# Layer-0 attention of a two-layer transformer: each head pair's projection and norm bound, and the ternary quantisation of the FFN weights, moved into the attention loops

## The reference

```
x = x + attn0(layernorm(x))   # qkv = x @ Wqkv.T + bqkv; 16 heads of 64; softmax(q k^T / 8) v; @ Wo.T + bo
x = x + ffn0(layernorm(x))    # gelu(x @ T(W1).T + b1) @ T(W2).T + b2
x = x + attn1(layernorm(x))   # Taylor feature map, causal
x = x + ffn1(layernorm(x))    # silu gate, int weights

def _ternary(w):              # T above; W1 is (4096, 1024), W2 is (1024, 4096)
    scale = jnp.maximum(jnp.mean(jnp.abs(w)), 1e-08)
    w_t = jnp.clip(jnp.round(w / scale), -1.0, 1.0)
```

## Time and profile before

| | us |
|---|---|
| median of 2 runs | 4363.91 (4304.0 to 4423.83) |
| the profiled execution, its own time | 4297.45 |
| its span on the slowest core (core 1) | 4295.9 |
| spans of the 8 cores | 4277.5 to 4295.9 |
| TensorE busy | 2523.8 (59%) |
| VectorE busy | 1594.5 (37%) |
| ScalarE busy | 1177.2 (27%) |

### The profile page before, as it was taken

One profiled execution on the slowest core, in us unless ns is written; L12 is line 12 of the kernel. 1 busy time (PEld: TensorE's weight loads), 2 busy tenths in 40 slices (PEclk: granted clock), 3 DMA queues, 4 the chain that ended last, 5 costly groups with the idle time before them and its releaser, 6 DMA issues. The chain is left out here.

```text
span 4295.9 us, 38629 instructions; the slowest of 8 cores (4277.5 to 4295.9 us)
## 1 busy us (share of the span) xinstructions
PE 2523.8 (59%) x12136; PEld 1064.5 (25%) x12136; DVE 1594.5 (37%) x3449; ACT 1177.2 (27%) x1691; POOL 110.4 (3%) x162
## 2 busy tenths in 40 slices
PE   1466565655656465000179996585555572779777
PEld 0112121121221112000034442243333340234333
DVE  2423324243232424645410003247777754231231
ACT  1162442615335162000231222213333332111110
POOL 0000000000000000111000000000000000001000
PEclk8687787867777687555589997785555576999999
DMA  4000000000000001756133321110000000636226
GB/s 113 8 1 8 0 8 8 0 8 1 8 0 1 0 1 69 262 193 201 57 88 74 74 59 20 30 20 1 1 1 1 1 1 7 87 59 75 45 39 123
DMA packets 178929, 188.11 MB, mean 44 GB/s; under 512 B 118432, under 2 KB 159408, under 8 KB 175024
## 3 DMA queue, kind: packets, MB, share of 16 engines
q0 software_dynamic: 90400, 126.92, 14.1%
q1 hardware_dynamic: 88336, 58.72, 4.9%
HBM read 211.85 MB, written 25.17 MB: 55 GB/s over the span
## 5 line engine op out<-in xcount | busy, mean ns | idle before, releaser
L52 ACT ACTIVATE SCR<-S,NEGC 128x1024 bf16<-128x1024 f32 x512 | 548.4, 1112 | 151.4 <-PE S L52 147.6
L52 PE MATMUL PO<-SCR,VP 128*65 128x512 bf16 x1024 | 346.5, 423 | 168.4 <-ACT SCR L52 92.8
L52 DVE CAST Y<-PO 64x512 bf16<-64x512 f32 x64 | 43.7, 683 | 630.1 <-PE PO L52 629.7
L52 DVE TENSOR_TENSOR X<-X,TF 128x512 f32<-128x512 f32 x64 | 44.3, 693 | 583.4 <-ACT TF L52 583.4
L52 PE MATMUL lnA<-lnXB,ONES_B 128*1 128x512 bf16 x128 | 56.8, 623 | 342.6 <-ACT lnXB L52 342.6
L52 PE MATMUL PGU<-XLN,WGS 128*128 128x512 bf16 x768 | 182.8, 381 | 119.0 <-DVE HH L52 93.7
L52 PE MATMUL PH<-XLN,W1S 128*128 128x512 bf16 x1024 | 223.0, 381 | 16.8 <-DMA W1S<-w1b 15.7
L52 PE MATMUL PH<-HSB,W2S 128*128 128x512 bf16 x1024 | 221.3, 379 | 1.9 <-ACT HSB L52 1.9
L52 PE MATMUL S<-QP,KP 64*128 64x512 bf16 x1024 | 216.4, 430 | 5.1 <-DVE NEGC L52 5.1
L50 DVE RECIPROCAL DROW<-DROW 1x512 bf16<-1x512 bf16 x64 | 206.6, 3292 | 0.8
L52 PE MATMUL PAUX<-DROW,ONES_B 1*64 1x512 bf16 x64 | 38.4, 599 | 284.7 <-DVE DROW L50 232.4
(11 more groups left out here) (157 smaller groups left out, 3787.5 us busy)
## 6 DMA issues: line engine op xcount, KB each, us to landing
WSL<-w POOLq DMA_DIRECT2D x16, 2048.0 KB, 11.6
WSL<-w POOLq DMA_DIRECT2D x64, 512.0 KB, 4.2
W1S<-w1b SPq DMA_DIRECT2D x16, 1024.0 KB, 5.3
W2S<-w2b SPq DMA_DIRECT2D x16, 1024.0 KB, 6.8
WGS<-wg POOLq DMA_DIRECT2D x12, 1024.0 KB, 8.9
WUS<-wu POOLq DMA_DIRECT2D x12, 1024.0 KB, 13.2
WDS<-wd POOLq DMA_DIRECT2D x16, 768.0 KB, 8.3
w1b<-WTB SPq DMA_DIRECT2D x8, 1024.0 KB, 4.5
```

What stands on the lines that cost most here:

```text
L52: ins = getattr(e, meth)(*a, **kw)
```

## The change

1. The steps ahead of the attention of a pair (projections, squares, norm matmuls, NEGC) become a generator `prep_chunks(pr)`, cut into 20 chunks: 8 for Q/K (one group each), 4 for V (four tiles each), 1 for the squares, 4 for the norms (four matmuls each), 3 for the chain to NEGC.
2. The ternary work becomes a generator `ternary_chunks()`: for each weight 8 chunks of four slabs of absolute sums, 3 for the threshold, 16 of two slabs of compare and write, 54 in all and a last empty one. W1 too is now cut into 32 slabs of 128x1024. Stage `p2a` is gone.
3. `pump()` appends one chunk to the engines' lists: of the next pair's preparation as long as there is any, else of the ternary work. It is called after each of the 17 steps of each `qc` block and after each of the 8 rounds of the tail, so 76 times a pair. Pair 0's own preparation is appended whole, ahead of the loop.
4. Everything that the chunks put into PSUM goes to the one bank PAUX; each use waits for VectorE's copy of the one before (`paux_free_vs`). The copies of Q and K move from ScalarE to VectorE. The squares get their own place in SCR, NEGC two buffers. The tail's broadcast matmuls use PO instead of PAUX.
5. The first block loads only pair 0's weights; pair pr + 1's are issued when the preparation of pair pr starts. WO0 is loaded inside `p2`, whose matmuls wait for it.

```diff
-    WO0 = sbuf("WO0", [128, 8 * 1024], BF16, es0a)
-    for i in range(2):
-        p.dma("gpsimd", WQP[i][:, :], dram["wq0"][i], dc)
...
+    p.dma("gpsimd", WQP[0][:, :], dram["wq0"][0], dc)
...
-    p.dma("gpsimd", WO0[:, :], dram["wo0"], dc)
...
+            def prep_chunks(pr):
                 pb = pr % 2
+                if pr + 1 < 8:
+                    p.wait("gpsimd", ts, trk["wread_ts"][1 - pb])
+                    p.dma("gpsimd", WQP[1 - pb][:, :], dram["wq0"][pr + 1], dwp[1 - pb])
...
+                for which in range(2):
+                    WB = WQP[pb] if which == 0 else WKP[pb]
...
                     for tc in range(NT):
+                        p.wait("tensor", vs, trk["paux_free_vs"])
                         for c in range(NFC):
+                            p.op("tensor", "matmul", PAUX[:, :], WB[:, c * 128:(c + 1) * 128],
                                  XLN[:, c * T + tc * 512: c * T + tc * 512 + 512],
...
+                        p.wait("vector", ts)
                         if which == 0:
+                            p.op("vector", "tensor_scalar", DSTT[:, tc * 512:(tc + 1) * 512],
+                                 PAUX[:, :], 0.125, BQ8[:, pr:pr + 1], AL.mult, AL.add,
+                                 inc=vs)
...
+                        trk["paux_free_vs"] = vs.n
+                        yield pr
                 for tt in range(NTT):
+                    p.wait("tensor", vs, trk["paux_free_vs"])
+                    p.op("tensor", "matmul", PAUX[:, 0:128], ONES_B[0:1, 0:128],
...
+                    trk["paux_free_vs"] = vs.n
+                    if tt % 4 == 3:
+                        yield pr
...
+                            p.wait("tensor", vs, trk["paux_free_vs"])
+                            p.op("tensor", "matmul", PAUX[0:1, 0:512], NRM2[:, aa:aa + 1],
...
+            def ternary_chunks():
+                w1q = dram["w1"].rearrange("c p (q f) -> c q p f", f=1024)
...
+                    nslab = 32
+                    p.wait("gpsimd", vs)
+                    p.dma("gpsimd", WSL[0][:, :], wdram(0), dsl[0])
+                    p.dma("gpsimd", WSL[1][:, :], wdram(1), dsl[1])
+                    for s_ in range(nslab):
+                        p.wait("vector", dsl[s_ % 2])
+                        p.op("vector", "reduce_sum", RACC[:, s_:s_ + 1], WSL[s_ % 2][:, :],
+                             axis=AX.X, apply_absolute_value=True, inc=vs)
+                        if s_ + 2 < nslab:
+                            p.wait("gpsimd", vs)
+                            p.dma("gpsimd", WSL[s_ % 2][:, :], wdram(s_ + 2), dsl[s_ % 2])
+                        if s_ % 4 == 3:
+                            yield 99
...
+                    for s_ in range(nslab):
+                        p.wait("vector", dsl[s_ % 2])
...
+                        if s_ % 2 == 1:
+                            yield 99
...
+            def pump(n=1):
+                for _ in range(n):
+                    if cur_prep[0] is not None:
+                        try:
+                            next(cur_prep[0])
+                            continue
+                        except StopIteration:
+                            cur_prep[0] = None
+                    if not tern_done[0]:
+                        try:
+                            next(tern)
+                        except StopIteration:
+                            tern_done[0] = True
+
+            for _ in prep_chunks(0):
+                pass
+
+            for pr in range(8):
+                pb = pr % 2
+                cur_prep[0] = prep_chunks(pr + 1) if pr + 1 < 8 else None
...
+                            exp_ss[(kt)] = ss.n
+                        pump()
+                    trk["last_exp_ss"] = exp_ss[NKT - 1]
...
+                        p.op("tensor", "matmul", PO[0:64, 0:512], ONES_B[64:65, 0:64],
                              DROW[64:65, g * 512:(g + 1) * 512], start=True, stop=True,
...
+                        p.op("vector", "tensor_mul", yslc, yslc, PO[0:64, 0:512], inc=vs)
+                        trk["zmul_vs"] = vs.n
+                        pump()
...
+            p.dma("gpsimd", WO0[:, :], dram["wo0"], dc)
+            p.wait("tensor", dc)
...
-    if act("p2a"):
```

More of the change, by code:

```diff
@@ L465, in build_program @@
                 sq_vs = vs.n
-                aux_v = vs.n
+                yield pr
                 p.wait("tensor", vs, sq_vs)
-                p.wait("tensor", vs, zmul_vs)
                 for which, SRC in enumerate([QS, KS]):
-                    for a in range(2):
+                    for aa in range(2):
                         for tc in range(NT):
[L472 to L476, removed]
+                            g = (which * 2 + aa) * NT + tc
+                            p.wait("tensor", vs, trk["paux_free_vs"])
+                            p.op("tensor", "matmul", PAUX[0:1, 0:512], NRM2[:, aa:aa + 1],
+                                 SRC[:, tc * 512:(tc + 1) * 512], start=True, stop=True,
+                                 inc=ts)
                             p.wait("vector", ts)
@@ L530, in build_program @@
                             if pk == 0:
[L531 to L535, removed]
+                                p.wait("tensor", vs, trk["o_evac_vs"])
+                                p.wait("tensor", vs, trk["zmul_vs"])
+                            for aa in range(2):
+                                p.op("tensor", "matmul", PO[:, aa * 512:(aa + 1) * 512],
+                                     VP[pb][:, pk * 130 + aa * 65: pk * 130 + aa * 65 + 65],
+                                     PSB[pk % 2][:, aa * 512:(aa + 1) * 512],
                                      start=(pk == 0), stop=(pk == NKT - 1),
-                                     inc=(ts if a == 1 else None))
+                                     skip_group_check=True,
+                                     inc=(ts if aa == 1 else None))
                             pv_ts[pk] = ts.n
@@ L564, in build_program @@
                 for qc in range(NT):
[L565 to L566 removed]
+                    for aa in range(2):
+                        g = qc * 2 + aa
                         p.wait("tensor", vs, zr_vs)
[L568 to L569 removed]
+                        p.wait("tensor", vs, trk["zmul_vs"])
+                        p.op("tensor", "matmul", PO[0:64, 0:512], ONES_B[64:65, 0:64],
                              DROW[64:65, g * 512:(g + 1) * 512], start=True, stop=True,
[L571 removed]
+                             skip_group_check=True, inc=ts)
                         zb_t = ts.n
                         p.wait("vector", ts, zb_t)
[L574 to L582 removed]
+                        yslc = Y[64 * aa:64 * aa + 64, pr * T + qc * 512: pr * T + qc * 512 + 512]
+                        p.op("vector", "tensor_mul", yslc, yslc, PO[0:64, 0:512], inc=vs)
+                        trk["zmul_vs"] = vs.n
+                        pump()
+                while cur_prep[0] is not None:
+                    pump()
+            while cur_prep[0] is not None or not tern_done[0]:
+                pump()
             p.emit(nc)
```

260 lines of the change are left out of this document (117 added, 143 removed).

## The result

| | before | after |
|---|---|---|
| median of all executions (10 and 11) | 4358.78 | 4492.34 |
| lowest | 4299.40 | 4357.28 |
| ratio, with its 95% interval | | 1.0135 (1.0117 to 1.0153) |
| the profiled execution, its own time | 4297.45 | 4395.29 |
| its spans over the 8 cores | 4277.5 to 4295.9 | 4331.8 to 4393.8 |

The change costs 1.35%, about 58 us, where +20 was forecast. That is within the 2% that were named as no change, but it is a loss, and the interval excludes none.

What follows compares the result with a forecast made beforehand. No engine bounds the whole: ScalarE's exponentials bound attention steps, the round trip through one bank the norms. Terms +5, -58, +22, +52, -17, +16 sum to +20 on 4295.9, 4317 us with 1.5 between span and time; range 4245 to 4390.

Steps and rivals of the forecast that it cites:

- Pairs 1 to 6: Preparation interleaved into the attention, with waits on one bank: +1 us a pair, +5 for six pairs (-46 to +50).
- the term V: V's four chunks between attention steps, on one bank: 18 or 26 us more by clock, 22 taken.
- Pair 0 and ternary: All ternary work falls into pair 0, with three attention blocks going under it: +52 us (+37 to +67).
- the term W1: In pair 0's ternary work, W1 in smaller slabs takes W2's 222 us instead of 155.0, 67 more.
- Pair 0's own preparation: Not interleaved and given one bank, so Q/K and V take longer: +22 us (+12 to +35).
- pair 7: The last pair has no next preparation to pump: -57.6 us.
- loads: First block loses WO0 and three weight slabs, so the layernorm starts earlier: -17 us (-10 to -20).
- `p2`: Output projection, where WO0's load now stands before the first matmul: +16 us (+13 to +20).
- some tens of us: Allowance on the total: a median of the changed kernel may lie up to this much above the 4317 us forecast.
- the round trips hide: Faster rival: interleaved chunks cost only their matmuls at full clock, 29 us less for each of seven preparations, 4114; 4%.
- the clock stays at half through the first block: Slower rival: Q/K and V steps run at half clock, +21 us over seven pairs, 4464; 7%.
- the slab loads slow down beside the attention: Slower rival: in pair 0 each of 128 ternary slabs takes 0.8 us longer, +102, 4419; 5%.

## Why the prediction was right or wrong

- **That interleaving hides almost nothing: right.** The list of TensorE is in order and every wait on PAUX stands in it. After the first, Q/K steps came at 2.83 to 3.04 us (2.84 forecast), the norms 1.52 apart (1.51), a pair at 188.6 (185). The forecast's reason, the round trip and not the matmuls, is shown by the run with everything on two banks.
- **Pairs 1 to 6, +5 forecast, +25 measured: the term V was mis-sized, and the three blocks behind the first were hardly priced.** "Four chunks are 18 or 26; take 22" was the mean of two clocks. The chunks with their steps took 29.3 us where 26.6 follow from the 22, with the last two steps at half clock and beyond it. Q/K took 24.3 with theirs, 1.2 more than forecast. In part this is hidden: its 17 steps were priced at 1.14 each, 19.4, where 21.3 was counted for the block, and the first block takes 80.4 where 78.8 follow from the forecast. The larger part is what follows the first block: the three others take 67.5 us for 63.4 with 1 forecast. They begin at half clock (0.50 over the first 8.3 us) and the chain to NEGC stands in the second; what each of the two costs was not measured apart. The argument for V leaned on gate/up, which is busy for 31.4 of 40 us and holds 1.00; a V tile of 0.77 us with 0.54 of wait isn't that case: the granted clock fell first during the fourth tile and stayed down from the eighth on (0.51 over the last 18 us of V), where the tiles came 1.77 apart.
- **Pair 0 and ternary, +52 forecast, +79 measured: the term W1 was mis-sized.** "W1 will now take W2's 222 as well" took the price from W2, whose slabs are written as one piece. W1's took 242.9, and the 21 us are its second pass, 4.27 us a slab for W2's 3.58; the sums ran at 3.08 us a slab, like W2's 3.03. The shape of the write was in the diff (the rearrangement with `f=1024`), and no row of before showed one. The run with the layout changed shows 13 to 17 of the 21; the run of before with 32 slabs shows the cost of the layout alone on four cores, and on the other four mostly together with the attention. The other 6 us are 3.3 in the chain (6.8 for 3.5) and 2.4 in W2 with the tail (256.4 for 254), which are not explained further. That all 54 chunks fall into pair 0, that VectorE waits for loads there and PO for VectorE: right.
- **Pair 0's own preparation** (+24.4 for +22), **pair 7** (-58.0 for -57.6), **loads** (-18.3 for -17) and **`p2`** (+14.3 for +16): right.
- **The range, 4245 to 4390,** holds the executions that the ratio compares (4357.3 to 4361.3) and not the median of all, 4492. The step that failed there is the allowance of "some tens of us" for the median: it lies 131 above the highest of these. The allowance was read off one median of two executions (4363.91); of eleven executions of after, eight lie at 4475.6 to 4571.7. Why more of them fall there than before, and further off, no run shows.
- **Rival "the round trips hide":** false for this kernel, true with one bank more. What it lacked was the condition.
- **Rival "the clock stays at half through the first block":** half true. V ran at half from its eighth tile on and the norms from the fourth, Q/K did not, so it cost about 4 us a pair and not 21. The granted clock of the block followed the waits: 0.69 with one bank, 0.81 with V on two, 0.98 with Q/K and the norms on two as well. The Trainium skill, "TensorE: Matmul & The Clock Gate", section "A second HAM failure mode: psum-queue depth-cycling", describes such an engine that pauses between groups of matmuls; here the trace agrees with it for the V tiles (0.51 over their last 18 us) and the norms (0.50 from the fourth on), and not for the Q/K groups (0.90 over all eight).
- **Rival "the slab loads slow down beside the attention":** false for the loads: the sums took 2.98 us a slab beside it and 2.92 without. The spaced writes of W1 were slower beside it on four of the cores (4.19 against 3.79 a slab), which the rival did not name.

## What to carry to other kernels

Work laid between the steps of another loop of an in-order engine costs its waits as well as its time, so give it the buffers that take the waits out first (here one bank: from 1.0135 to 0.9625), and price both the waits and the clock that they cost. Feed side work at the pace at which it is ready, across all iterations, rather than as soon as there is a free place: the same ternary work held pair 0 for 586 us when it was taken greedily, and for 192 when it was spread, at up to 11 us more for a later pair. When a tile of a transfer is cut smaller, look at the pitch of both ends, not at its bytes alone.

## What the runs showed of the hardware

- A write of 256 KB as 128 rows of 2 KB took 2.0 to 2.4 us to land (medians of the cores) with the rows one behind the other, and 2.7 to 4.2 with the rows 8 KB apart. Whether the pitch does it or only that the rows don't touch, no run shows. The reads did not show it: W1's slabs are read as rows of 4 KB at a pitch of 16 KB and came at 2.98 us a slab, W2's, in one piece, at 3.04 (means of the cores). The Trainium skill, "DMA: Bandwidth & Descriptors", section "Latency and other measured facts", gives rates for row pitches at large powers of two from 512 KB on (207 GB/s there, 164 at 2 MB); no run here has such a pitch, and these runs show a loss at 8 KB, for writes.
- The reduces of 1x512 out of PSUM start 0.61 and 0.70 us apart in turn when they alternate between two banks, though each is recorded as 0.67 to 0.68 long; with one bank the same operation came each 1.31 us before the clock fell and each 1.52 at half clock.
